# Pieces stored three rows to a channel, small transfers reordered, and small work moved behind the main work of each step

## The reference, cut to what matters

```python
# layer 0: ordinary softmax attention, 16 heads of 16 channels
xn = layer_norm(x, norm_w, norm_b)
q, k = heads(xn @ q_w + q_b), heads(xn @ k_w + k_b)
att = softmax(q @ k^T + (1 - mask) * -1e6)          # over keys, per batch and head
y = att @ heads((xn @ v_w + v_b) * mask)
scale, shift = split(silu(cond) @ emb_w + emb_b)
x = x + silu(layer_norm(y) * (1 + scale) + shift) @ out_w + out_b
# layer 1: linear attention, 8 heads of 32 channels
q = softmax over channels; k = softmax over tokens (with the mask); att = k^T v; y = q att
x = x + silu(layer_norm(y) * (1 + scale) + shift) @ W_out + b_out
```

## Time and profile before

| what | us |
|---|---|
| median of three runs | 725.44 |
| the profiled execution | 723.0 |
| its span, first to last instruction | 721.2 |
| PE (TensorE matmul) busy | 579.2 (80%) |
| DVE (VectorE) busy | 441.6 (61%) |
| ACT (ScalarE) busy | 351.3 (49%) |
| POOL (GpSimd) busy | 65.9 (9%) |
| mean granted TensorE clock | 0.891 of full |

### The profile page before, as it was taken

The page is one execution under the profiler, slowest core; times in us unless marked ns, Lnnn a source line. Parts: engine busy times, 40 slices in busy tenths (PEclk is TensorE's granted clock), DMA queues, the critical chain, the costliest instruction groups (busy, mean ns, idle before and its releaser), DMA issues.

```text
span 721.2 us, 7870 instructions
## 1 busy us (share of the span) xinstructions
PE 579.2 (80%) x2938; PEld 264.8 (37%) x2938; DVE 441.6 (61%) x891; ACT 351.3 (49%) x408; POOL 65.9 (9%) x85
## 2 busy tenths in 40 slices
PE   2608830899989988999998899999897999984875
PEld 1203510323334332434433333445333443333574
DVE  5134540457766896778788588777954788304443
ACT  0310200555556667565666656565545756671431
POOL 1021040000000003010001012000050101000300
PEclk9955855699999997999999799999966999997897
DMA  6143384003341000211102000000000000000001
GB/s 177 53 117 123 119 243 138 21 1 109 108 145 70 18 24 1 69 41 29 47 22 69 12 13 23 1 24 30 24 0 24 30 30 1 2 0 1 0 1 59
DMA packets 19494, 36.40 MB, mean 50 GB/s; under 512 B 3528, under 2 KB 10400, under 8 KB 19424
## 3 DMA queue, kind: packets, MB, share of 16 engines
q1 hardware_dynamic: 19264, 35.85, 16.7%
q10 hardware_dynamic: 192, 0.05, 0.0%
HBM read 20.76 MB, written 14.96 MB: 50 GB/s over the span
## 4 chain that ended last, share of the span: by engine, by line
PE 52%; DVE 17%; DMA 13%; ACT 6%; issue 4%; SPq 4%; ACTq 1%; POOL 0%; POOLq 0%; DVEq 0%
PE bank L849 13%; DMA stack_rows<-late 11%; DVE halfmax L972 10%; PE sT L830 9%; PE bank L738 8%; PE bank L717 8%; SPq L430 3%; PE bank L790 2%; PE sT L717 2%; PE bank L752 2%; DVE stats L903 2%; ACT prob L678 2%; DMA qs<-crows 2%; ACT hT L617 2%; PE bank L759 1%
## 5 line engine op out<-in xcount | busy, mean ns | idle before, releaser
L972 DVE TENSOR_REDUCE halfmax<-bank 128x1 f32<-128x512 f32 x512 | 325.3, 684 | 151.0 <-PE bank L738 149.5
L678 ACT ACTIVATE prob<-sT 128x1024 f32<-128x1024 f32 x256 | 257.4, 1023 | 185.2 <-PE sT L830 184.8
L738 PE MATMUL bank<-ks,qs 50*128 50x512 f32 x512 | 159.1, 455 | 42.7 <-DMA qs<-stack_rows 21.3
L830 PE MATMUL sT<-qs,ks 52*128 52x512 f32 x512 | 132.2, 507 | 45.4 <-DMA qs<-crows 34.5
L849 PE MATMUL bank<-prob,vp 128*17 128x512 f32 x1024 | 143.3, 633 | 4.2 <-ACT prob L678 4.2
L830 PEld LDWEIGHTS sT<-qs,ks 52*128 52x128 f32 x512 | 50.6, 192 | 178.6 <-issue 98.9
L738 PEld LDWEIGHTS bank<-ks,qs 50*128 50x128 f32 x512 | 73.0, 200 | 92.6 <-DVE halfmax L972 63.9
L534 POOL TENSOR_TENSOR rstd<-var,neghalf 128x4 f32<-128x4 f32 x14 | 14.2, 1015 | 591.8 <-DVE var L913 591.8
L717 PE MATMUL bank<-w,hT 128*128 128x256 f32 x144 | 39.1, 409 | 0.5
L849 PEld LDWEIGHTS bank<-prob,vp 128*17 128x17 f32 x1024 | 17.2, 96 | 43.9 <-issue 32.4
L717 PEld LDWEIGHTS bank<-w,hT 128*128 128x128 f32 x144 | 26.8, 202 | 9.0 <-DVE halfmax L972 3.5
(11 more groups left out here) (130 smaller groups left out, 461.0 us busy)
## 6 DMA issues: line engine op xcount, KB each, us to landing
stack_rows<-late SPq DMA_DIRECT2D x32, 256.0 KB
ks<-stack_rows SPq DMA_DIRECT2D x16, 400.0 KB
qs<-stack_rows SPq DMA_DIRECT2D x32, 192.0 KB, 3.4
stack_rows<-late SPq DMA_DIRECT2D x8, 512.0 KB
out_x<-xs SPq DMA_DIRECT2D x4, 512.0 KB, 3.0
xs<-in_x SPq DMA_DIRECT2D x4, 256.0 KB, 3.9
xs<-in_x SPq DMA_DIRECT2D x2, 512.0 KB, 6.5
late<-in_L_cond_emb_w SPq DMA_DIRECT2D x1, 1024.0 KB, 11.2
```

Of the source, the lines that this page charges most:

```text
L678: act.activation(prob[:, c % 2, 2 * u:2 * u + 2, :].rearrange("p j n -> p (j n)"), sT[u][:, :], ACT.Exp).then_inc(exp_done, 1)
L738: last = pe.matmul(o, qs[rows, s % SLOTS, c, t * P:(t + 1) * P], ks[rows, hg, c, half * HALF:(half + 1) * HALF], start=True, stop=True)
L830: last = pe.matmul(sT[u][:, two * HALF:(two + 1) * HALF], ks[rows, hg, u, c * P:(c + 1) * P], qs[rows, s % SLOTS, u, :], start=True, stop= ...
L972: dve.tensor_reduce(halfmax[:, s % 2, r, half:half + 1], o, axis=AX.X, op=ALU.max, negate=True).then_inc(u.done, 1)
```

## The change

1. **Layout in DRAM.** `stack_rows` goes from [group, head side, 50 rows, token] to [group, 128 channels, 3 pieces, token]. A group is stored by four DMAs, each over 64 channels, in place of five over 4 or 8 heads of 16 rows. Keys load 48 rows from it (before: 50, with the mask rows).
2. **Mask and ones.** The mask rows no longer pass through `stack_rows`: SyncE writes them straight into `ks` for batch 0 at the start, and with each `load_keys` of batch 1. The ones come in runs of 1024 elements in place of 128, out of a corner of the tile `prob` that GpSimd fills.
3. **Queues.** The 17 small loads move from ScalarE's queue to SyncE's, ahead of the first `store_parts`. After the third group's loads SyncE now goes: store group 3, load its keys, embw, `load_max(0)`, and then bias rows, wo0, w1.
4. **Steps.** The half-steps' work is issued together behind scores(k, 1) and its maxima. On ScalarE both exponentials come first, then `copy_values`, then the rest. "y" goes from half-step 2·NT·(s+1)+1 to +2, and with it layer norm "mid0" starts one step later.

```diff
-            at["y", s] = 2 * NT * (s + 1) + 1
+            at["y", s] = 2 * NT * (s + 1) + 2
...
-        stack_rows = nc.dram_tensor("stack_rows", [G, 2 * GH, ROW_MAX, T], F32, kind="Internal").ap()
+        stack_rows = nc.dram_tensor("stack_rows", [G, P, PIECES, T], F32, kind="Internal").ap()
...
-            for b in range(B):
-                sp.dma_start(stack_rows[b * HG:(b + 1) * HG, GH:2 * GH, ROW_MASK:ROW_MAX, :].rearrange("g x r n -> g x (r n)"),
-                             mask_rows[b].rearrange("r n -> (r n)").unsqueeze(0).unsqueeze(0).to_broadcast([HG, GH, PARTS * T])).then_inc(fill_in, 16)
+            for two in range(2):
+                rows = slice(two * TILE + ROW_MASK, two * TILE + ROW_MAX)
+                sp.dma_start(ks[rows, :, :, :].rearrange("r g c x -> r (g c) x").bitcast(F32), mask_rows[0].unsqueeze(1).to_broadcast([PARTS, HG * 2, T])).then_inc(rows_in, 16)
+            for at_row in (0, 32):
+                for i, src in enumerate((v_b, bq, bv)):
+                    sp.dma_start(braw[at_row:at_row + 1, i, :], src.rearrange("(o d) -> o d", o=1)).then_inc(braw_in, 16)
+            for name, src, n in (...):
+                loads(sp, name, src, n, vecs2, NV0, vec2_in)
...
-                for xs_of, r, piece in ((slice(0, 2 * GH), 0, 0), (slice(0, GH), 1, 0), (slice(GH, 2 * GH), 2, 0), (slice(0, GH), 2, 1), (slice(GH, 2 * GH), 1, 1)):
-                    sp.dma_start(stack_rows[g, xs_of, r * DH0:(r + 1) * DH0, :], parts[xs_of.start * DH0:xs_of.stop * DH0, g % 2, piece, :]).then_inc(parts_out[g % 2], 16)
+                for side, both, single in ((1, 0, 2), (0, 1, 0)):
+                    rows = slice(side * GC, (side + 1) * GC)
+                    sp.dma_start(stack_rows[g, rows, both:both + 2, :], parts[rows, g % 2, :, :]).then_inc(parts_out[g % 2], 16)
+                    sp.dma_start(stack_rows[g, rows, single, :], parts[rows, g % 2, 0, :]).then_inc(parts_out[g % 2], 16)
...
-                    sp.dma_start(ks[two * TILE:two * TILE + ROW_MAX, g % HG, :, :].bitcast(F32),
-                                 stack_rows[g, GH + 2 * two:GH + 2 * two + 2, :, :].rearrange("c r n -> r c n")).then_inc(k_in[g % HG], 16)
+                    src = stack_rows[g, GC + two * GC // 2:GC + (two + 1) * GC // 2, :, :].rearrange("(c p) r n -> (p r) c n", c=2)
+                    sp.dma_start(ks[two * TILE:two * TILE + ROW_MASK, g % HG, :, :].bitcast(F32), src).then_inc(k_in[g % HG], 16)
+                    if g >= HG:
+                        sp.dma_start(ks[two * TILE + ROW_MASK:two * TILE + ROW_MAX, g % HG, :, :].bitcast(F32),
+                                     mask_rows[g // HG].unsqueeze(1).to_broadcast([PARTS, 2, T])).then_inc(k_in[g % HG], 16)
...
                 exponential(k, 0)
-                for key in act_at[k, 0]:
-                    take(key)
+                exponential(k, 1)
                 if c == 0 and s > 0:
                     copy_values(s - 1)
-                exponential(k, 1)
-                for key in act_at[k, 1]:
+                for key in act_at[k]:
                     take(key)
...
                 if k > 0:
                     values(k - 1)
-                for key in pe_at[k, 0]:
-                    fill(key)
                 scores(k, 1)
                 for key in maxima(k, 1):
                     fill(key)
-                for key in pe_at[k, 1]:
+                for key in pe_at[k]:
                     fill(key)
```

More of the change, by code:

```diff
@@ L254, in two_layer_conditioned_attention @@
         projections(1, 0, max(first, last))
[L256 to L261, removed]
+        pe_at, act_at, dve_mid, dve_at = ({k: [] for k in range(STEPS + 2)} for _ in range(4))
+        begins = {key: i // 2 for key, i in sorted(at.items(), key=lambda item: item[1])}
@@ L262, in two_layer_conditioned_attention @@
+        for key, k in begins.items():
+            assert k < STEPS
+            pe_at[k].append(key)
             if key[0] == "qk":
[L263 to L264 removed]
+                act_at[k].append(key)
+                dve_mid[k + 1].append(key)
             elif key[0] in ON_ACT:
[L266 removed]
+                act_at[k].append(key)
             else:
[L268 removed]
+                dve_at[k].append(key)
@@ L275, in two_layer_conditioned_attention @@
-        dve_at[later(begins["values", 0, 3], 4)].append(("recips", 0))
+                dve_at[k + 2].append(("qsum", key[1], key[2] // 2))
+        dve_at[begins["values", 0, 3] + 2].append(("recips", 0))
         for (kind, b, h), k in layer_at.items():
             for i in range(QT):
-                dve_at[k, i // 2].append(("stats", kind, b, h, i))
-            dve_at[k + 1, 0].append(("aggr", kind, b, h))
+                (dve_mid if i < 2 else dve_at)[k].append(("stats", kind, b, h, i))
+            dve_mid[k + 1].append(("aggr", kind, b, h))
@@ L352, in two_layer_conditioned_attention @@
         in_ring = [key for key in pe_beside if key[0] in ("max", "neg")]
-        for spot in spots:
-            in_ring += (maxima(*spot) if spot[0] < STEPS else []) + pe_at[spot]
+        for k in range(STEPS):
+            in_ring += maxima(k, 0) + maxima(k, 1) + pe_at[k]
         in_ring.append(("y", SUBS - 1))
@@ L358, in two_layer_conditioned_attention @@
         act_order, taken = [], {key: i - len(dve_order) for i, key in enumerate(dve_order)}
-        for i, spot in enumerate(spots):
-            now = (maxima(*spot) if spot[0] < STEPS else []) + [key for key in dve_at[spot] if key in whole]
-            also = [key for key in act_at[spot] if key in whole and key[0] in ON_ACT]
+        for k in range(STEPS + 2):
+            now = [key for key in dve_step(k) if key in whole]
+            also = [key for key in act_at[k] if key in whole and key[0] in ON_ACT]
             for j, key in enumerate(now + also):
-                taken[key] = 16 * i + j
+                taken[key] = 16 * k + j
             dve_order += now
@@ L1080, in _ @@
                 take(key)
-            for k in range(STEPS):
-                for p in range(2):
-                    for key in maxima(k, p):
-                        take(key)
-                    for key in dve_at[k, p]:
-                        take(key)
-            for spot in spots[2 * STEPS:]:
-                for key in dve_at[spot]:
+            for k in range(STEPS + 2):
+                for key in dve_step(k):
                     take(key)
```

97 lines of the change are left out of this document (46 added, 51 removed).

## The result

The changed kernel takes 676.04 us (median of 4 runs, 672.07 to 678.77) against 724.37 for the kernel before (4 runs, 720.7 to 726.71): ratio 0.933, 95% interval 0.927 to 0.940. In a second set of runs it took 671.95 against 722.75, ratio 0.930 (0.927 to 0.932). Predicted were 680 us, 660 to 702.

The account below looks back on a forecast made before the run. TensorE was taken to bound the ring, and SyncE's chain of slow stores the start. From 723.0, less 41.3 for the start, 2 for clock, 2 for waits and 0 for order, 677.7; with 2.4 to the median, 680, range 660 to 702.

Parts of the forecast that it names:

- First store issued, 26.0: In the start, the first store can be issued at 26.0 us, before 28.3, with the bias rows next late.
- 8 was named as a sign: In the start, ScalarE would wait some 8 us for the first store in place of 14.4.
- First store, 7.5 us: In the start, the first store takes 7.5 us from first issue to landing, before 16.9.
- Rival (a): Stores use sixteen engines but run at 183 GB/s; 29.3 us gained in the start, 692 us; chance 0.16.
- First loads, 9.85 us unchanged: In the start, the loads behind the first store still take 9.85 us, since more engines do not make them faster.
- Maxima to row, 38.5: In the start, first maxima to the row of maxima takes 38.5 us, before 41.0, as VectorE's wait shrinks by 2.5.
- SyncE's chain and `load_max(0)`: In the start, SyncE's transfers run beside the maxima; `load_max(0)` issued at 82, its bytes behind embw, scores at 87.5.
- the sum of 41.3: The start's gain: scores begin at 87.5 us against 128.8, so 41.3 us gained.
- Clock at the ring's start, −2: In the ring's first steps, a shorter TensorE wait gives back at best 2.4 us of granted clock, zero at worst.
- Waits for transfers in the ring, −2: In the ring of 128 steps, four `load_max` waits of 3.4 us shrink, giving 2 us.
- Step order, 0: In the ring, the new order of the steps changes nothing, with ends of −15 and +12 us.
- Rival (c): In the ring, the order starves VectorE of banks; with `copy_values` 50 us lost, about 730 us; chance 0.04.

Follow-up runs that it names:

- e6: The changed kernel with the 17 small loads behind the first store in SyncE's list and VectorE's bias row work behind six lo pieces: 669.01 us, ratio 0.926.
- e7: As e6, with `load_max(0)` also ahead of the 2 MB of embeddings in SyncE's list: 664.87 us, ratio 0.921.
- e1: The kernel before with the new DRAM layout alone, mask rows written straight into `ks`, old queues and step order: 684.76 us, ratio 0.948.
- e4: The changed kernel with the stores' outermost size back at 4 heads, same bytes and same four DMAs: 737.1 us, ratio 1.021.
- a1: The changed kernel unaltered, run again on another chip: 671.95 us, ratio 0.930.
- e2: The kernel before with the new queues alone, old layout and step order: 714.43 us, ratio 0.989.
- e3: The kernel before with the new step order alone: 727.13 us, ratio 1.0053.
- e5: The changed kernel with the old step order: 677.06 us, ratio 0.937.
- e8: As e9, with the old step order: 672.07 us, ratio 0.929.
- e9: As e7, with the 17 small loads on ScalarE's queue behind its fourth hi piece: 665.17 us, ratio 0.921.
- e11: As e9, with `copy_values` ahead of the second exponential again: 665.11 us, ratio 0.919.

## Why the prediction was right, step by step

- *First store issued, 26.0:* 26.86. The bias rows landed at 23.3 (22 to 23.5 forecast) and were next late, with VectorE 11.7 us idle before them; e6 and e7 show it by taking them away (19.41 and 18.54). ScalarE did start early, at 11.28 (about 11 forecast), but then waited 13.78 us for the first store, where 8 was named as a sign and 14.38 had been.
- *First store, 7.5 us:* 8.8. The mis-sized term: 16 engines, but 212 GB/s, near the low row (183) and not the high one. The four issues under it took 4.2 us and not 2, and no byte moved in the first 1.1. Rival (a) had the rate nearly right; it failed in what followed. It had 16 us for a store and its loads, where they took 12 to 13 (35.65, 48.42, 60.30, 73.60 are the asks for keys).
- *First loads, 9.85 us unchanged:* 8.96 (8.8 in e1, 8.9 in e4, 8.1 in a1; 10.1 in e2, whose keys are 50 rows). So the new layout gives some 1 us here. The rule of the Trainium skill above (DMA: Bandwidth & Descriptors) points the same way, 10 engines to 16, but the prediction's estimate from it was a third, some 3 us. What of the 1 us is the engines', and what the other order of rows in DRAM or the 4% fewer bytes of the keys, was not tried.
- *Maxima to row, 38.5:* 35.7. The term for the wait was right: a1 has 38.3 at a clock of 0.72 there, near the 0.71 of the kernel before. The other 2.6 us go with the clock, which the forecast left alone: 0.79 in the changed kernel's profile (31.2 us for the 87 matmuls in place of 34.9), and in e6 0.86 with 33.5 us.
- *SyncE's chain and `load_max(0)`:* issued 80.4 (82), scores at 86.35 (87.5), with embw in front of it, 4.4 us of TensorE's time. In a1 the row is there 2.5 us later and TensorE waits 1.3 us, with scores at 85.7 all the same: the two paths do end together. Errors of +0.9, +1.3, −0.9 and −2.8 met here; the sum of 41.3 came out as 42.4. That they cancelled so well is partly luck.
- *Clock at the ring's start, −2:* wrong. From 88 to 96 the clock is 0.50 and TensorE does 30 matmuls, as in the earlier trace rows. A wait of 4 us in place of 31 did not spare it that, nor did one of 1.4 in e7 (0.50 and 30 matmuls from 80 to 88).
- *Waits for transfers in the ring, −2:* ScalarE's 3.4 us went; TensorE's waits for `load_max` are 3.4 as before. e1's ring is 516.2 against 520.5. Of the 4 us of this term and the one before, the changed kernel's ring shows 2.2 in its first profile (518.3) and, with the step order in it, 8.8 in a1's (511.7): one profile cannot tell terms of this size.
- *Step order, 0:* wrong in size, inside its ends. On the kernel before it costs 4 us (e3); with fast stores it gives 5 to 7 (e5, e8). Part of that is clock. A straight line through the runs of each pair, time against granted clock, leaves some 3 us at equal clock (e8's two runs at 0.916 took 672.04 and 672.09, e9's one 669.22). It is not saved waiting: in the new order TensorE is idle longer in the ring in all three pairs (a1 and e5 44.1 and 39.2 us, e9 and e8 43.8 and 39.3, e3 and the kernel before 49.1 and 41.0), and its matmuls are shorter by 8.4, 6.5 and 5.1. Why the same matmuls take less time, and why the new order is granted more clock, stays open. Rival (c)'s 50 us, VectorE short of banks, did not come; `copy_values` costs nothing that can be told (e11).

## What to carry to other kernels

Look at the DMA share before counting bytes: here a share of 0.23 to 0.25 under a transfer that was alone said that its outermost size kept it on four engines, and the layout with 64 channels outermost was worth 36.6 of the start's 42.4 us. Once such a wait is gone, the small transfer that had been hidden behind it is the next bound: move it behind the first use of the freed time, and look what waits for it in its new place (in e9, VectorE's statistics). An order written out by hand has to change on all engines at once; half of it cost 33 us here, where the whole gives 5 to 7. And compare kernels at equal granted clock where the difference is of a few us.

## What the hardware showed that was not expected

Stores from 64 partitions by 16 engines at a share of 0.90 moved 212 GB/s, while an output tile over 128 partitions moved 348; which difference (partitions, the length of the runs in DRAM, four DMAs in place of one) makes it was not tried. And TensorE's clock is at 1.2 GHz (0.50) in the ring's first steps after an idle of 1.4 us (e7) or 4 as after one of 31. In the changed kernel it was granted in full from 60 to 72 us and was at a mean of 0.66 from 74.5 to 80, where TensorE still made maxima at VectorE's pace: the low level had begun before the idle did.
